# Moving the query projection ahead of P times V, and its copy from VectorE to ScalarE, in the attention stage with sinks

## The reference, cut to what matters

```
NQ, NKV, HD, SW = (32, 8, 64, 64)          # query heads, key heads, head size, masked band
proj = x @ W_qkv
q, k, v = jnp.split(proj, (NQ * HD, (NQ + NKV) * HD), axis=-1)
q = _apply_rope(q...); k = _apply_rope(k...)
attn = einsum('bqhmd,bkhd->bhmqk', q, k) / 8
mask = (q_pos >= k_pos) & (q_pos < k_pos + SW);  attn = where(mask, -inf, attn)
w = softmax(concatenate([attn, sink], -1))[..., :-1]
out = einsum('bhmqk,bkhd->bqhmd', w, v).reshape(B, L, NQ * HD)
return out @ W_out
```

## Time and profile before

| | |
|---|---|
| median of 3 runs | 4607.78 us (4607.42 to 4613.61) |
| profiled execution, its own time | 4608.71 us |
| span of that execution's trace | 4607.0 us |
| loop of the first sequence, first to last even or odd `values` | about 2051.3 to 2308.7 us |
| loops of the other three | from 2369.9, 2687.3 and 3004.8 us |

### The profile page before, as it was taken

One profiled execution on the slowest core, in us unless ns is written; L12 is line 12 of the kernel. 1 busy time (PEld: TensorE's weight loads), 2 busy tenths in 40 slices (PEclk: granted clock), 3 DMA queues, 4 the chain that ended last, 5 costly groups with the idle time before them and its releaser, 6 DMA issues. The chain is left out here.

```text
span 4607.0 us, 78083 instructions
## 1 busy us (share of the span) xinstructions
PE 3628.7 (79%) x22008; PEld 2850.1 (62%) x22011; DVE 2893.3 (63%) x6445; ACT 2178.2 (47%) x5590; POOL 1719.1 (37%) x2974
## 2 busy tenths in 40 slices
PE   7799849449988749449999999999647499999464
PEld 3455537337766637337777777777545388888443
DVE  5799666545444466558868768688363566667452
ACT  3799414225544414147757767577212344445111
POOL 0499525532222225535435445355147000000155
PEclk9799959769888859769999999999856699999666
DMA  2011214410000214420000000000324200000424
GB/s 77 30 49 46 98 69 139 114 37 1 0 1 1 101 52 138 112 70 18 17 9 18 16 11 18 11 15 18 123 63 65 89 1 1 2 2 1 161 41 100
DMA packets 133855, 222.84 MB, mean 48 GB/s; under 512 B 28656, under 2 KB 107248, under 8 KB 131648
## 3 DMA queue, kind: packets, MB, share of 16 engines
q1 hardware_dynamic: 99728, 148.95, 9.6%
q0 software_dynamic: 33792, 69.83, 6.9%
HBM read 163.71 MB, written 54.80 MB: 47 GB/s over the span
## 5 line engine op out<-in xcount | busy, mean ns | idle before, releaser
L1256 POOL DMA_INDIRECT ex_xr<-scratch_rows,mo_token x288 | 286.7, 996 | 347.5 <-issue 175.8
L598 POOL TENSOR_TENSOR sc_h<-sc_h,sc_c 128x512 f32<-128x512 f32 x256 | 327.2, 1292 | 194.7 <-DVE sc_h L635 186.8
L2727 DVE TENSOR_TENSOR sa_pT<-bank,sa_pT 128x512 fp32r<-128x512 f32 x512 | 329.9, 686 | 79.6 <-ACT sa_pT L2594 75.7
L2586 ACT ACTIVATE sa_p<-bank,sa_nm 128x512 f32<-128x512 f32 x512 | 346.5, 688 | 45.2 <-DVE sa_nm L2718 45.2
L2445 PE MATMUL bank<-sa_pT,sa_v 128*128 128x256 f32 x2048 | 310.8, 294 | 70.0 <-DVE sa_pT L2727 69.2
L635 DVE TENSOR_TENSOR_SCAN sc_h<-sc_da,bank 128x512 f32<-128x512 f32 x256 | 311.1, 1220 | 38.2 <-ACT sc_da L578 23.3
L2421 PE MATMUL bank<-sa_kT,sa_qT 128*128 128x512 f32 x1024 | 332.9, 436 | 1.5 <-DVE residual L2694 1.5
L2445 PEld LDWEIGHTS bank<-sa_pT,sa_v 128*128 128x128 f32 x2048 | 257.9, 188 | 113.8 <-DVE sa_pT L2727 112.2
L2714 DVE TENSOR_REDUCE sa_mx<-bank 128x2 f32<-128x1024 f32 x256 | 312.5, 1221 | 18.0 <-PE bank L2423 15.0
L2594 ACT ACTIVATE sa_pT<-bank 128x512 fp32r<-128x512 f32 x512 | 274.2, 585 | 95.3 <-PE bank L2433 94.6
L1322 PE MATMUL bank<-mo_w_gu,ex_xT 128*128 (+2 forms) x1152 | 312.9, 400 | 1.3 <-ACT ex_xT L1370 0.7
(11 more groups left out here) (372 smaller groups left out, 10021.4 us busy)
## 6 DMA issues: line engine op xcount, KB each, us to landing
scratch_ys<-ex_yo SPq DMA_DIRECT2D x192, 128.0 KB, 2.0
mo_w_gu<-in_w_gu SPq DMA_DIRECT2D x2, 9216.0 KB, 25.5
sc_c<-scratch_c SPq DMA_DIRECT2D x64, 256.0 KB, 3.1
sa_share<-scratch_shares SPq DMA_DIRECT2D x256, 64.0 KB, 2.6
mo_w_dn<-in_w_dn SPq DMA_DIRECT2D x2, 4608.0 KB, 47.2
mo_w_dn<-in_w_dn SPq DMA_DIRECT2D x2, 4096.0 KB, 33.4
scratch_rows<-ln_stage POOLq DMA_DIRECT2D x64, 128.0 KB, 5.2
ex_xr<-scratch_rows,mo_token POOLq DMA_INDIRECT x288, 2.8
```

What stands on the lines that cost most here:

```text
L598: pool.tensor_tensor(h, h, C[u], ALU.mult).then_inc(used.sem, 1)
L1256: pool.indirect_dma_start(xr[u][:, :], None, rows, bass.IndirectOffsetOnAxis(ap=token[:, i:i + 1], axis=0), bounds_check=rows.shape[0] - 1 ...
L2586: act.activation(pr[h][:, :], SC[2 * s_ + h][:, :], ACT.Exp, bias=nm[:, col:col + 1], scale=SCALE, accum_out=rs[:, col:col + 1]).then_inc( ...
L2727: dve.tensor_tensor(spot(1), PT[h][:, :].rearrange("p (k n) -> p k n", k=TPB), spot(0).bitcast(F32), ALU.subtract).then_inc(*inc("kept_d"))
```

## The change

PE calls `project(q+2)` ahead of `values(N-2)` instead of behind it. The copy `fetch_q` goes from DVE's program to ACT's: there it stands at the head of an even step, ahead of `low_y`; ahead of the loop it stands behind `keep_keys` of tile 0 and behind `keep_q` of the first quad. Its waits (`qp`, `qput`) are the same. Nothing else differs.

```
@@ PE, steps
                             scores(g, p)
+                            if s_ == 0 and (qt + 2 < QUADS or not last):
+                                project(q + 2, *((g, qt + 2) if qt + 2 < QUADS else (g + 1, qt + 2 - QUADS)))
                             if p >= 2:
                                 values(N - 2, g, p - 2, 0)
                             elif not first:
                                 values(N - 2, g, p - 2 + STEPS_, 1)
-                            if s_ == 0 and (qt + 2 < QUADS or not last):
-                                project(q + 2, *((g, qt + 2) if qt + 2 < QUADS else (g + 1, qt + 2 - QUADS)))
@@ ACT
+                def fetch_q(q):
+                    act.wait_ge(*at("qp", q + 1))
+                    if q:
+                        act.wait_ge(*at("qput", q))
+                    act.activation(qraw[:, :], QB[:, 0:QW], ACT.Copy).then_inc(*inc("qraw"))
@@ ACT, steps
                             if s_ == 1 and (qt + 1 < QUADS or not last):
                                 keep_q(q + 1, qt + 1)
+                            if s_ == 0 and (qt + 2 < QUADS or not last):
+                                fetch_q(q + 2)
                             if p >= 2:
                                 low_y(N - 2, p - 2)
@@ ACT, ahead of the loop
                         if i >= 1:
                             keep_keys(b, i - 1)
+                        if i == 1:
+                            fetch_q(b * G * QUADS)
                     keep_keys(b, TPB - 1)
                     keep_q(b * G * QUADS, 0)
+                    fetch_q(b * G * QUADS + 1)
                     groups(steps)
@@ DVE
-                def fetch_q(q):
-                    dve.wait_ge(*at("qp", q + 1))
-                    if q:
-                        dve.wait_ge(*at("qput", q))
-                    dve.tensor_copy(qraw[:, :], QB[:, 0:QW]).then_inc(*inc("qraw"))
@@ DVE, steps, and its two calls ahead of the loop
-                            if s_ == 0 and (qt + 2 < QUADS or not last):
-                                fetch_q(q + 2)
```

More of the change, by code:

```diff
@@ L2784, in _ @@
                         low_v(b, i)
-                        if i == 1:
-                            fetch_q(b * G * QUADS)
                         if b and i >= 1:
                             add_out(b - 1, i - 1)
-                    fetch_q(b * G * QUADS + 1)
                     if b:
```

## The result

The changed kernel takes 4527.99 us, median of 4 runs (4524.26 to 4530.27). On the same chip the kernel before took 4608.2 us. The ratio is 0.9823, 95% interval 0.9806 to 0.984: faster by 80 us. The profiled execution of the changed kernel took 4524.26 us, against 4608.71 before.

What follows compares the result with a forecast made beforehand. A ring of waits through PE, ACT and DVE was taken to bound each 8.20 us quad. 0.69 us less in 116 quads gives 80, plus 1 at the loop heads: 4608.71 becomes 4528 us, range 4512 to 4558.

Steps and rivals of the forecast that it cites:

- The projection out of the ring: Projection no longer delays `turn_p`: start of even to start of odd `values` falls from 4.39 to 3.60 us (3.55 to 3.66).
- the ring: Chain of waits through PE, ACT and DVE, without slack, taken to set the 8.20 us quad; the projection stood inside it.
- The projection in front of V: From odd to next even `values`, the projection ahead makes PE come last: 3.91 us (3.81 to 4.07), against 3.81.
- The copy onto ACT: ACT's copy at the even step's head fills idle ahead of `low_y`: 0.40 us, slack 0.4, cost 0; uncovered, 46 us.
- The copy off DVE: DVE's 0.41 us copy was hidden by a 0.63 wait for ACT; taking it off gains 0 by itself.
- Who is served earlier: Copy ready 0.8 us after the even `values` start, not 2.42, for `turn_q` and POOL's `put_q`, ending at 4.6 to 5.2.
- the slower rival: POOL's late `put_q` steps delay DVE's negation and `add_y` 0.8 us a quad: 93 us lost, 4620; chance 0.04.
- The heads of the loops: Ahead of the loops PE waits less for the copy; 1 us taken off at the first, net gain 1 us.
- PE's own work binds more than I think: Only PE's shown idle ahead of the even `values`, 0.49 us a quad, can be won: gain 57, 4551; chance 0.2.
- The ring still comes last: PE passes from mask to `values` 0.1 us faster, so the chain of waits binds: quad 7.41, 4516; chance 0.13.
- The copy delays ACT: Late projection result or `qput` holds ACT's queue with `low_y` and `high_p`; 0.3 us too late loses 35: 4563; chance 0.05.
- no change: Something else of 8.2 us closes the quad's wait chain, such as the row's way through SP and DMA; chance 0.03.

Runs made afterwards that it cites:

- 3: Kernel before with only the projection's copy moved to ACT, behind `low_y`, PE's order unchanged: 4605.26 us, ratio 0.9994.
- 6: Changed kernel with 2 of the 6 matmuls of each projection in the loop, low-part products left out: 4519.37 us, ratio 0.9809.
- 9: Changed kernel with the reciprocals' transpose ahead of the odd `values` and DVE's `invert` ahead of `low_p`: 4527.5 us, ratio 0.9807.
- 5: Changed kernel with three projection matmuls done once more ahead of the projection: 4579.15 us, ratio 0.9933.
- 7: Changed kernel with one more ACT copy of the same size ahead of the loop's copy: 4523.85 us, ratio 0.9813.
- 8: Changed kernel with two extra ACT copies ahead of the loop's copy, the second after a semaphore from the first: 4551.57 us, ratio 0.9871.
- 2: Kernel before with only the projection's copy moved to ACT, at the head of the even step, PE's order unchanged: 4653.23 us, ratio 1.009.
- 1: Kernel before with only the projection moved ahead of `values`, its copy staying on DVE behind `add_y`: 4591.69 us, ratio 0.996.
- 4: Kernel before with the six projection matmuls done once more ahead of the even `values`, the real projection staying in place: 4610.41 us, ratio 1.0006.
- 11: Changed kernel with only ACT's row copy moved behind the odd `high_p`, `add_y` waiting for the transpose instead: 4522.48 us, ratio 0.9808.
- 10: Changed kernel with the early transpose and `invert`, plus ACT's row copy behind the odd `high_p` and `add_y` waiting for the transpose: 4504.32 us, ratio 0.9771.

## Why the prediction was right, point by point

*The projection out of the ring* (V to W 3.60 between 3.55 and 3.66): 3.57 at V 2772.72. The running ahead of the weight loads, for which 0.06 of a possible 0.1 was taken, gives 0.09: V to `turn_p` is 0.96, and 1.05 wherever the ring comes last at V (experiments 3, 6, 9). The weight loads of V's group show the same step on PEld, before and after:

```profile
2810.34 1.01 PEld L2445 LDWEIGHTS bank<-sa_pT,sa_v 128*128 128x128 f32 x8 [0.62 <-DVE sa_pT L2727]
2772.61 1.03 PEld L2445 LDWEIGHTS bank<-sa_pT,sa_v 128*128 128x128 f32 x8
```

Before, the first load starts with its matmul (2810.34); after, 0.11 ahead of it (2772.61 against 2772.72). The limit that the prediction set here was wrong, and did no harm: with `low_y` fixed at V + 1.25 and ACT free at V + 1.65, V to W could not have fallen below 3.63. But `low_y` waits for the end of the same `values`, came earlier with it, at V + 1.16, and `high_p` started at V + 1.60.

The Trainium skill, TensorE: Matmul & The Clock Gate, LDWEIGHTS, had served here as the ground for an estimate of 107 ns a matmul and 90 us of gain; the six matmuls ahead of V take 0.79 from start to start (2771.93 to 2772.72), 0.13 each, and the gain was 80, so the row of before was the better price, and the estimate from the page's figure too low for these matmuls.

*The projection in front of V* (W + 3.91): 3.91 in the quad shown and 3.93 in the median, but with two of its terms off by as much in opposite ways. From mask to projection it was 0.04 to 0.05, not 0.09: a mask twice as wide (2771.88 to 2771.93) costs no more than the narrow one of the earlier trace rows: the projection's first matmul starts 0.05 behind the mask's start, though the mask's row lasts 0.29. From projection to `values` it was 0.79, not 0.73. The 0.73 was read behind `values` and ahead of the transposes; ahead of `values` the same six take longer, and the earlier trace rows gave only their start. The scores' 1.95 and 1.14 were 1.96 and mostly 1.12 to 1.15. That the sum came out to the hundredth is partly luck; that PE comes last by 0.1 was right, and it is confirmed by (5) and by the missing bracket ahead of V.

*The gain of 0.69 in 116 quads, 80 us*: the loops show 80.8.

*The copy onto ACT at no cost*: right. It started at V + 0.27, not V + 0.40. The exponential's `sa_es` ended at W + 4.31, as said (2773.09, with the W before at 2768.78), but the copy started 0.10 before that end (2772.89 + 0.20 against 2772.99), and this V came at W + 3.94. The slack was 0.51 instead of 0.4. Experiments 7 and 8 show its size. The 0.40 without cover is what 2 measured (0.38 a quad and 43 us; 46 was said).

*The copy off DVE, a gain of 0*: right, by 3. But this term needs the word "by itself". With the projection moved it is the copy's place on DVE that holds PE (1): of the 80 us, the order gives 19 alone and the copy's move 0 alone. The two parts aren't a sum, and the prediction priced them together without saying so.

*Who is served earlier*: POOL's last step of `put_q` ended at V + 5.00, between 4.6 and 5.2, and 0.6 ahead of the V + 5.6 from which the slower rival would have begun. The small negation stays within the 0.62 that was named as a bound: 160/182/622 ns in the profile after against 160/373/624 in the earlier trace rows. In this quad POOL's last step had only 0.11 left when it started, and it took 0.16.

*The heads of the loops, net 1 us*: the gaps between the loops lost 3.6, not 1.5. Two of the three lost 0.6 and 0.7 and the middle one 2.3; the second profile of the change shows the same three gaps. What the middle one won I haven't traced, and its cause stays open. Whether the 1 taken off at the first loop was right can't be told: the first `values` came at 2052.1 in one execution of the change and at 2047.7 in the other, against 2051.3 before.

*The rivals.* "PE's own work binds more than I think" is refuted by 4, and by the result. "The ring still comes last" was nearer than its chance of 0.13 suggests: the ring's 3.81 and 3.66 make 7.47, PE's road 7.48 in the quad shown and 7.50 in the median, and experiments 6 and 9 run into the ring at once. The page of the Trainium skill that the prediction names led to that case through a faster load; what brings it about instead is any small saving on PE. "The copy delays ACT" begins half a us later (8). "Slower" and "no change" didn't occur.

## What to carry to other kernels

When a ring of small waits through several engines sets the time, look which work in it belongs to another period, and put it where the engine would stand waiting anyway; but look who reads the result, for the reader's place in its own queue must move with it, or the wait only moves there (1 against the change). A test inside the trace (here the quad without a projection) prices such a move better than the busy shares do. Once two roads are equally long, judge a further edit by what both become: one saving alone shows nothing, both together do (9 and 11 against 10).

## What the runs showed of the hardware

The idle that the profile shows ahead of a waiting matmul is less than the work that fits there: 0.49 us was shown, and six matmuls of 0.80 us together fit there for 0.6 us a loop of 257 (experiment 4). The difference lies in the mask ahead, whose 0.23 us still counts as busy when nothing holds up a follower that starts 0.04 behind it, and in the stream: a group of eight `values` hands over to the next after 0.96 us when it follows without a gap and after 1.05 when PE had waited ahead of it (2772.17 to 2773.22 in 9), which returns 0.09 of the 0.1 us by which PE was late.

A negation of 128x2 on DVE took 0.16 us in this quad and 0.56 in the kernel before, at the same place. Before, POOL's step L2252 had 0.55 to go when it started (2815.99 against 2815.81 + 0.73), after only 0.11 (2777.61 against 2776.98 + 0.74). The rest of the two traces says the same: each of the 512 negations took 0.16 us, or until 0.015 us behind the end of the POOL instruction that was running when it started, whichever was longer. In 119 of them before, L2252 had 0.49 left in the median; in 109 after, 0.10. No run was made for this alone, so the cause is argued from the timelines. It agrees with the Trainium skill, SBUF — State Buffer, SBUF: two separate sides, by which such a pair excludes each other.
